# Moving the next tile's K/V/Q pieces earlier in the attention loop of a transformer layer on eight cores

## The reference

```python
x = x + _layernorm(attn(_layernorm(x), Wq, Wkv, Wproj))
x = x + _layernorm(ffn(_layernorm(x), w1, b1, w2, b2))

def attn(x, Wq, Wkv, Wproj):      # 16 heads of 64, 4 KV heads, window 512
    q, (k, v) = x @ Wq.T, split(x @ Wkv.T)
    q, k = q/(norm(q)+1e-6), k/(norm(k)+1e-6)     # per head
    q, k = rope(q), rope(k)
    mask = (cols <= rows) & (cols > rows - 512)
    attn = softmax(where(mask, q k^T / 8, -inf))
    return (attn @ v) @ Wproj.T

def ffn(x, w1, b1, w2, b2):       # 1024 -> 4096 -> 1024
    return relu(x @ w1 + b1) @ w2 + b2
```

## Time and profile before

| | |
|---|---|
| runs | 4638.1 and 4662.94 us, median 4650.52 us |
| profiled execution | 4640.36 us |
| its span, slowest core (core 5) | 4638.8 us |
| spans of the eight cores | 4622.6 to 4638.8 us |
| mean granted TensorE clock of the cores | 0.717 to 0.721 |
| stage A on core 5 | up to 2782 us (tile 31's store is issued at about 2782 us) |
| stage B | the rest |

### The profile page before, as it was taken

One profiled execution on the slowest core, in us unless ns is written; L12 is line 12 of the kernel. 1 busy time (PEld: TensorE's weight loads), 2 busy tenths in 40 slices (PEclk: granted clock), 3 DMA queues, 4 the chain that ended last, 5 costly groups with the idle time before them and its releaser, 6 DMA issues.

```text
span 4638.8 us, 50340 instructions; the slowest of 8 cores (4622.6 to 4638.8 us)
## 1 busy us (share of the span) xinstructions
PE 2627.3 (57%) x15808; PEld 1265.5 (27%) x15808; DVE 1746.8 (38%) x4530; ACT 1261.0 (27%) x4001; POOL 9.4 (0%) x21
## 2 busy tenths in 40 slices
PE   2444555455454444554544554777666777777776
PEld 1222333233232222332332331222222222222222
DVE  2343334334334343343343332333333333333333
ACT  1343444444343444444443440000000000000000
POOL 0000000000000000000000000000000000000000
PEclk8566666666666665656666657888888888888888
DMA  7000000000000000000000013000000000000000
GB/s 134 19 10 19 10 10 10 19 10 10 19 10 14 14 10 19 10 10 19 10 10 19 10 30 71 19 19 19 19 19 19 19 19 19 19 19 19 19 19 19
DMA packets 20723, 93.12 MB, mean 20 GB/s; under 512 B 2336, under 2 KB 2352, under 8 KB 19056
## 3 DMA queue, kind: packets, MB, share of 16 engines
q1 hardware_dynamic: 18432, 67.12, 4.2%
q0 software_dynamic: 2032, 22.79, 2.9%
HBM read 78.89 MB, written 33.55 MB: 24 GB/s over the span
## 4 chain that ended last, share of the span: by engine, by line
PE 43%; DVE 24%; issue 13%; ACT 8%; DVEq 6%; DMA 4%; ACTq 2%; SPq 0%; POOL 0%; POOLq 0%
PE psO L714 6%; DVE sb_aT L573 6%; PE ptr L682 5%; DVEq L797 5%; PE psX L714 5%; DVE sb_hT L686 5%; PE pjq L365 5%; PE pjq L634 3%; PE psAV L591 3%; PE ptr L563 3%; DMA sb_xt<-x 3%; PE psE L696 3%; DVE sb_st L253 2%; ACT sb_junk L515 2%; ACTq L797 2%
## 5 line engine op out<-in xcount | busy, mean ns | idle before, releaser
L563 PE MATMUL ptr<-sb_ident,sb_E 128*128 128x128 bf16 x2240 | 295.7, 282 | 724.6 <-DVE sb_aT L573 721.5
L686 DVE TENSOR_SCALAR sb_hT<-ptr,sb_b1f 128x128 bf16<-128x128 bf16 x1024 | 290.5, 284 | 523.0 <-PE ptr L682 522.1
L682 PE MATMUL ptr<-sb_ident,sb_hT 128*128 128x128 bf16 x1024 | 232.3, 227 | 409.9 <-DVE sb_hT L686 242.0
L276 PE MATMUL ptr<-sb_ident,sb_ln 128*128 128x128 bf16 x512 | 64.7, 306 | 639.2 <-DVE sb_ln L270 594.6
L563 PEld LDWEIGHTS ptr<-sb_ident,sb_E 128*128 128x128 bf16 x2240 | 181.8, 122 | 817.4 <-issue 808.0
L591 PE MATMUL psAV<-sb_aT,sb_VR 128*64 128x128 bf16 x2240 | 323.2, 300 | 86.4 <-DVE sb_aT L573 86.0
L573 DVE COPY sb_aT<-ptr 128x640 bf16<-128x640 bf16 (+4 forms) x720 | 263.1, 365 | 241.8 <-PE ptr L563 216.0
L682 PEld LDWEIGHTS ptr<-sb_ident,sb_hT 128*128 128x128 bf16 x1024 | 101.1, 99 | 752.5 <-issue 752.4
L696 PE MATMUL pjq<-sb_warena,sb_lt 128*128 128x512 bf16 x1024 | 298.3, 394 | 1.3 <-DVE sb_lt L282 1.3
L262 ACT ACTIVATE sb_st<-sb_st,sb_epsc 128x1 f32<-128x1 f32 x128 | 37.7, 294 | 912.9 <-DVE sb_st L258 912.9
L714 PE MATMUL psO<-sb_warena,sb_hT 128*128 128x512 bf16 x1024 | 281.9, 444 | 0.0
(11 more groups left out here) (124 smaller groups left out, 4315.0 us busy)
## 6 DMA issues: line engine op xcount, KB each, us to landing
sb_xt<-x SPq DMA_DIRECT2D x32, 512.0 KB, 4.2
sb_warena<-w POOLq DMA_DIRECT2D x8, 2048.0 KB, 46.6
x1s<-sb_x1t SPq DMA_DIRECT2D x32, 512.0 KB, 2.8
sb_x1t<-x1s SPq DMA_DIRECT2D x32, 512.0 KB, 3.8
y<-sb_xt SPq DMA_DIRECT2D x32, 512.0 KB, 2.9
sb_warena<-wq POOLq DMA_DIRECT2D x1, 2048.0 KB, 26.2
sb_warena<-wp POOLq DMA_DIRECT2D x1, 2048.0 KB, 38.5
sb_warena<-wkv POOLq DMA_DIRECT2D x1, 1024.0 KB, 14.5
```

Source lines behind the costliest of these rows:

```text
L563: E("pe", lambda e, eb=eb, jj=jj, slot=slot: e.transpose(ptr[:, slot * 128:(slot + 1) * 128], eb[:, jj * 128:(jj + 1) * 128], ident[:]), r ...
L682: E("pe", lambda e, m=m, slot=slot: e.transpose(ptr[:, slot * 128:(slot + 1) * 128], hTb[:, m * 128:(m + 1) * 128], ident[:]), reads=(f"{h ...
L686: E("dve", lambda e, m=m, slot=slot: e.tensor_scalar(hTb[:, m * 128:(m + 1) * 128], ptr[:, slot * 128:(slot + 1) * 128], b1f[:, m:m + 1], ...
```

## The change

The chunks of the next tile are put at other places among the head pairs. Before, the chunks listed for c ran behind pair_phase2(c-1); now they run ahead of pair_phase1(c), and the list is shifted so that chunk 0 is ahead of pair 0 and chunk 6 ahead of pair 6. Nothing is computed in another way, and no buffer changes.

```diff
-            sched = {1: [0], 2: [1], 3: [3], 4: [4], 5: [5], 6: [2]} if INTERLEAVE else {}
+            sched = {0: [0], 1: [1], 2: [3], 3: [4], 4: [5], 5: [2], 6: [6]}                 if INTERLEAVE else {}
             prev = None
             if not NOPAIRS:
                 for c in range(8):
+                    for k in sched.get(c, []):
+                        if k < len(kvq):
+                            kvq[k]()
                     heads = pair_phase1(c)
                     if prev is not None:
                         pair_phase2(prev[0], prev[1])
-                    for k in sched.get(c, []):
-                        if k < len(kvq):
-                            kvq[k]()
                     prev = (c, heads)
                 pair_phase2(prev[0], prev[1])
-                if INTERLEAVE:
-                    if len(kvq) > 6:
-                        kvq[6]()
-                else:
+                if not INTERLEAVE:
                     for chunk in kvq:
                         chunk()
```

## The result

The changed kernel takes 4757.6 us (median of 12 executions) against 4643.4 us (10 executions) for the kernel before. The ratio is 1.0228, 95% interval 1.0189 to 1.0268: slower by 2.3%, where 1.5 to 1.7% was forecast and 4665 to 4770 us was the range.

A forecast was written before the change was run, and what follows sets the result against it. The attention stage was taken as bound by a chain hopping between engines. Terms 1.19 + 0.52 + 0.91 - 0.42 + 0.40 = 2.60 us a tile, 80.6 us over 31 tiles, on 4640.4 gave 4721 us; range 4665 to 4770.

The forecast's parts named there:

- Step 1: Front of the tile: kv_mms waits for VectorE's lt copy, holding up the scores of pair 0; +1.19 us a tile.
- Step 2: Front of the tile: kv_mms loses the faster clock, 3.57 us in place of 3.05; +0.52 us a tile.
- Step 3: Gap after pair 4: qT_tr, hidden in the tail before, is no longer hidden; +0.91 us a tile.
- Step 4: Between pair_phase1(0) and (1): k_chain costs 1.45 us against 1.87 in its old gap; -0.42 us a tile.
- Step 5: Tail: the projection starts colder, without about 1 us of TensorE work just before it; +0.40 us a tile.
- (a): Rival: clock goes fully against the change in q_halves and projection, k_chain gains nothing; 3.94 us a tile, 4763 us; chance 0.23.
- (b): Rival: the clock repays the change through faster q_halves and projection; -0.45 us a tile, 4626 us; chance 0.10.
- (c): Rival: kv_mms at the front keeps the upper clock all tile; -3.8 us a tile, 4522 us; chance 0.04.
- (d): Rival: earlier start pays, k_chain and qT_tr hidden; 0.24 us a tile, 4648 us; chance 0.11, with mixtures of gains.

The follow-up runs named there:

- Experiment 5: The kernel before, with only the scores of pair 0 also waiting for the next tile's lt copies: 4719.7 us, ratio 1.0163.
- experiment 1: The kernel before, with kv_mms alone moved ahead of pair_phase1(0) and its old gap left empty: 4725.8 us, ratio 1.0181.
- experiment 2: The kernel before, with kv_mms ahead of pair_phase1(0) and k_chain between pair_phase1(0) and (1): 4727.7 us, ratio 1.0195.
- Experiment 3: The changed kernel with qT_tr alone put back at the end of the pairs: 4713.5 us, ratio 1.0165 to the kernel before.
- experiment 8: The kernel before, with the matmuls of kv_mms and both q_halves inside pair_phase2 of pairs 0, 1 and 2: 4354.6 us, ratio 0.9375.
- experiment 4: The kernel before, with kv_mms moved ahead of pair_phase1(0) and run again in its old gap after pair 0: 4829.2 us, ratio 1.0411.
- experiment 7: The kernel before, with kv_mms moved between pair_phase1(0) and pair_phase1(1): 4547.3 us, ratio 0.980.

## Why the prediction was right where it was, and where it was wrong

The direction, the range and the places were right. The size was about two thirds of what was measured: 2.60 us a tile forecast, 3.64 us measured in full tiles (92.32 us, where 91 to 92 was forecast). That it stayed in the range is in part luck: three terms were too low by 1.1, 0.4 and 0.4 us, and the q_halves, taken at nothing, gave 0.7 us back.

- **Step 1, the wait for lt: right in itself.** 38.2 us over 32 waits, 1.19 us each, as forecast from the earlier trace rows. Experiment 5 shows that its effect on the kernel is over twice that (2.66 us a tile), through the clock of pair 1.
- **Step 2, kv_mms and the clock: mis-sized, the main error.** The term was +0.52 us; kv_mms itself did lengthen by 0.58 us (2.93 to 3.51), and 3.57 us is what it takes in tiles of the changed kernel at a clock of 0.50. What the step left out is that the faster clock was no property of kv_mms alone: it carried the scores, transposes and psAV matmuls after it. Leaving the gap saved 1.89 us (experiment 1), where the step counted 3.05. Moving kv_mms cost 4.65 - 1.89 = 2.8 us where steps 1 and 2 together had 1.71.
- **Step 3, qT_tr: right.** 0.82 us for 0.91.
- **Step 4, k_chain: wrong by 0.4 us.** The new price was right (1.45 forecast, 1.42 measured in experiment 2), the old one not (1.87 against 1.40). The base for it took 0.54 us from psAV's end to L511, read at 1106.91 to 1107.45, right behind kv_mms, where the clock was up (1.00 in that window). In the changed kernel, at 0.50, the same way takes 0.85 us (1092.92 to 1093.77), which makes the old price 1.56. The segments say it directly: 7.84 with, 6.44 without.
- **Step 5, the projection: mis-sized.** +0.40 forecast, as half of the distance to the last tile's 5.83 us; it was +0.75 (5.75 us), nearly all of it. The reason given, that work just before it is gone, does not hold as it stands: 10 of the 23 tiles have 5.16 us without that work, and 13 have 6.27 us, more than the bound of 5.83. The q_halves, taken at 0, gave 0.7 us back in their segments, in 12 of those 13 tiles. Experiment 3 shows that both come and go with the place of qT_tr. So the two terms are one pattern of the clock, worth 0.1 us a tile on balance, and the prediction had them as two.
- **Sum.** 2.8 (kv_mms) + 0.0 (k_chain) + 0.8 (qT_tr) + 0.8 (tail) - 0.7 (q_halves) = 3.7 us, against 3.64 measured. Over 31 tiles that is 113 us; stage A on core 1 ends 110.7 us later (2771.4 to 2882.1).
- **Rivals.** (a) gave 4763 us, nearer to the outcome than the forecast, but for partly other reasons: the projection came out as in (a), the q_halves the other way, k_chain with no gain as in (a), and the clock lost around kv_mms was in none of the rivals. (b) and (c) fell: the mean clock of stage A fell from 0.62 to 0.59. (d) fell too: k_chain costs 1.42 us in its new place and qT_tr 0.82 us, so neither was hidden.
- **The clock.** At the front, behind long idling, kv_mms takes 3.2 to 3.6 us (3.51 in the mean), and where experiment 8 fills the waits of pairs 1 and 2 the granted clock is 1.00 and 0.93 in the mean. The Trainium skill, page "TensorE: Matmul & The Clock Gate", section "Why this matters for your kernels", advises to keep TensorE busy without gaps to get and hold the full clock. The two agree with it.

What stays open: why the clock rises while kv_mms runs in the kernel before (22 of 23 tiles) and only at its end or later once the tile's work comes 1.2 us later (20 of 23), and why the changed kernel has two kinds of tiles. The rows show that it is so, and not by what rule. A comparison that keeps the clock fixed was not to be had.

## What to carry to other kernels

Where TensorE works in short bursts between waits, a burst's price is not its length: time the whole segment around it with and without it, since the clock that it raises may shorten its neighbours, and a wait of 1 us elsewhere can lose that. When a chunk has to share an in-order queue with a chain, put it where that engine waits for another, in pieces of one engine's work only; a chunk that makes a second engine wait ahead of the chain's next step keeps its price. Filling TensorE's waits paid twice here, in cover and in clock: the three matmul chunks went from 7.8 us a tile (1.89 for kv_mms, 2.78 and 3.13 for the q_halves over an empty pair) to none.

## What the runs showed of the hardware

- A wait of 1.2 us in each of 31 tiles, with nothing else changed, made the kernel 78 us slower (ratio 1.0163), 41 us beyond its own length: the granted clock over the segment of pair 1, which became 1.22 us longer a tile, fell from 0.91 to 0.71.
- kv_mms in the same place took 2.4 to 2.9 us in most tiles of the kernel before and 3.6 us in most tiles of experiment 5; a q_half, also eight matmuls of 512 columns, took 1.89 us in experiment 8.
- A pair with eight extra matmuls of 512 columns inside it (5.76 us in the mean, clock 0.93) was faster than a pair without them (6.44 us, clock 0.50); at 1.00 it took 5.55 us, at 0.73 or 0.74 it took 6.34 us (experiment 8).
- Within one execution of the changed kernel the same 16 matmuls of the projection took 6.27 us in 13 full tiles (clock of the tail 0.64) and 5.16 us in 10 (0.80).
- In some kernels full tiles keep nearly one length (standard deviation 0.26 to 0.33 us in experiments 4, 7 and 8), in the others less so (0.6 to 1.45 us, the most in experiment 5).
